# A layer of causal attention and gated FFN on 8 cores: squares moved to GpSimd, dequant jobs moved and paced anew inside attention, three output tiles moved to VectorE

## The chip, the cores and the metric

The kernel runs on the 8 cores of one Trainium2 chip. Each core takes one of 8 batch entries and computes it alone; no core talks to another. The metric is the device time in microseconds (us) of the slowest core. The engines are called PE (TensorE), DVE or VectorE, ACT or ScalarE, POOL or GpSimd, and SP (SyncE), which only issues DMAs here.

## The reference

```python
# per batch entry: x is [2048, 1024]
xn = layernorm(x)
q, k, v = xn @ Wq, xn @ Wk, xn @ Wv        # 16 heads of 64; rope on q and k
attn = softmax(causal(q @ k.T / 8))
s = (attn @ v) @ Wo
h = layernorm(xn) * gamma + beta
w1 = (fc1_q - 128) * fc1_scales            # int32 [1024, 4096], a scale per 128 rows
w2 = (fc2_q - 128) * fc2_scales            # int32 [4096, 1024]
f = xn + 0.5 * (silu(h @ w1 + b1) @ w2 + b2)
out = x + s * silu(f)
```

## The kernel before

The program is written as five blocks, b0 to b4, one after the other. In each block a small scheduler (`Sched`) keeps a list of instructions for every engine; `sch.op` adds one, `sch.wait` adds a wait for a semaphore count. Every engine executes its list strictly in the order in which the Python code has added to it, so the place of a call in the code is the place in the queue of each engine that it touches.

**b0 and b1** load constants, build the rope tables, compute the statistics of the rows and write the transposed, normalized input `xn_fm` (bf16).

**b2** projects. First V, while GpSimd multiplies (`emit_h_mul`, L397) and VectorE scales (`emit_h_ts`, L405) the eight slices of h. Then Q and K in eight slabs `it` (four each). A slab has four quarters `tgq` of 512 positions. For a quarter PE runs 16 matmuls (L558, L563), ACT copies both results out of PSUM (L574, L576), and VectorE does six rope instructions of 128x512 bf16 (L582 to L597), the first behind a wait for the copies of the slab before. At the slab's end ACT issues eight DMAs that place the result in `q_att` or `k_att` (L609, L612). The softmax needs a bound on the scores, for which the squared norms of each slab are summed. `emit_norm_sq(it-1)` puts the square of the first half of the slab before on ACT (L499), waiting for its eight DMAs, ahead of everything that ACT does for slab `it`. After quarter 1 of slab `it`, `emit_norm_mm(it-1, 0)` and `(it-1, 1)` follow: four PE matmuls with a vector of ones (L519), a VectorE reduce and maximum (L525, L533), for the second half first another square (L512). There is one buffer `nsq_b` and one PSUM bank for it, so the second square waits for the first norm's matmuls, and the second norm's matmuls wait for VectorE's maximum of the first. Quarters 2 and 3 stand behind them in PE's queue. After slab 7 the same is done with nothing beside it.

**b3** is attention, then the output projection and half of the first FFN matmul. Attention runs 32 groups: `qg` 0 to 3 (512 queries each) times `m` 0 to 7 (two heads each), with K = 4 qg + 4 key tiles. For each key tile `kt`, `emit_scores_exp` adds two score matmuls (L759), one exp on ACT (L778), and for the last four key tiles GpSimd's masks (memsets L788, multiplies L790). `emit_av(kt-2)` adds the matmuls with V (L808) and those that sum the softmax's denominators (L816); they wait for the masks. A group's epilogue has two parts. `ep_a` is two reciprocals of 1x512 (L829) and two casts (L834) on VectorE; it is added at kt = 1 of the next group. `ep_b` is two PE matmuls (L841), a copy (L849) and a multiply (L853) on VectorE; it is added at the end of the next group.

Beside attention the FFN weights are dequantized, in 48 jobs: 16 for w1 (2048 columns) and 32 for w2 (1024 columns). `emit_dq_job` adds two loads on SP, one scalar_tensor_tensor on VectorE (STT, L714), which waits for the loads and for the store of the job before, and the store on GpSimd (L719), which waits for the STT. All jobs use one set of buffers. At the end of each group, behind the epilogue of the group before, jobs are added until `want` are done; `gidx` is the number of groups added so far:

```python
                        if gidx <= 12:
                            want = min(ndq, gidx // 3)
                        else:
                            want = min(ndq, 4 + (gidx - 12) * (ndq - 4) // 20)
                        while dq_next < want:
                            emit_dq_job(dq_next)
```

**b4** does the second FFN matmul in two passes of eight row tiles (tile tt = 0 to 7 and 8 to 15) and, ahead of the second pass, the other half of the first FFN matmul (L1070, with Silu on ACT, L1078). For each row tile: PE's 64 matmuls (L1100, L1104), loads of x and s by SP (L1116, L1118), which wait until the two tiles before are computed (`o_done`), four VectorE instructions (L1125 to L1136), Silu on ACT (L1143), a multiply and an add, and the store issued by ACT. The multiply and the add are on GpSimd for tt < 13 (L1151, L1154) and on VectorE for 13 to 15 (L1159, L1162). The x tile and the result have two buffers each; the s tile has one.

Of the kernel before, what the change touches and what calls it, by code (L numbers as in the profile page):

```python
# [7 lines left out]
F32 = mybir.dt.float32  # L8
BF16 = mybir.dt.bfloat16
I32 = mybir.dt.int32  # L10
AF = mybir.ActivationFunctionType
# [3 lines left out]
S = 2048  # L15
D = 1024
# [77 lines left out]
def build_nc(upto=9):  # L94
# [31 lines left out]
    with ExitStack() as es:  # L126
# [5 lines left out]
        def sb(stack, name, cols, dt):  # L132
            return stack.enter_context(nc.sbuf_tensor(name, [128, cols], dt))
# [36 lines left out]
        with ExitStack() as ps:  # L170
# [4 lines left out]
            sch = Sched(cts)  # L175
# [51 lines left out]
        with ExitStack() as ps:  # L227
# [7 lines left out]
            sch = Sched(cts)  # L235
# [130 lines left out]
        with ExitStack() as ps:  # L366
# [5 lines left out]
            sch = Sched(cts)  # L372
# [78 lines left out]
            nsq_b = sb(ps, "nsq_b", S, BF16)  # L451
# [7 lines left out]
            dr_rep = {}  # L459
# [26 lines left out]
            sc_nsq = {}  # L486
            pe_nmm = {}
            ve_nrm = {}

            def emit_norm_sq(itx):  # L490
                ti_x, cp_x = itx // 4, itx % 4
                att_x = q_att if ti_x == 0 else k_att
                for j2 in range(2):
                    im = 8 * ti_x + 2 * cp_x + j2
                    m = 2 * cp_x + j2
                    if im >= 1:
                        sch.wait("scalar", "cPE", pe_nmm[im - 1])
                    sch.wait("scalar", f"dR{itx % 2}", dr_rep[(itx, 3)])
                    sch.op("scalar", lambda e, att_x=att_x, m=m: e.activation(  # L499
                        nsq_b[:], att_x[:, S * m:S * (m + 1)], AF.Square), inc="cSC")  # L500
                    sc_nsq[im] = sch.snap("cSC")
                    break

            def emit_norm_mm(itx, j2):
                ti_x, cp_x = itx // 4, itx % 4
                att_x = q_att if ti_x == 0 else k_att
                im = 8 * ti_x + 2 * cp_x + j2
                m = 2 * cp_x + j2
                if j2 == 1:
                    if im >= 1:  # L510
                        sch.wait("scalar", "cPE", pe_nmm[im - 1])
                    sch.op("scalar", lambda e, att_x=att_x, m=m: e.activation(  # L512
                        nsq_b[:], att_x[:, S * m:S * (m + 1)], AF.Square), inc="cSC")
                    sc_nsq[im] = sch.snap("cSC")
                sch.wait("tensor", "cSC", sc_nsq[im])
                if im >= 1:
# [22 lines left out]
            for ti, (w_d_, att) in enumerate(((wq_d, q_att), (wk_d, k_att))):  # L539
                for cp in range(4):  # L540
# [65 lines left out]
                    for j in range(4):  # L606
                        h = 4 * cp + j
                        m, r = h // 2, 64 * (h % 2)
# [40 lines left out]
        with ExitStack() as ps:  # L649
# [25 lines left out]
            with ExitStack() as ds:  # L675
# [46 lines left out]

                dq_next = 0
                sc_exp = {}
                pe_avl = {}
# [8 lines left out]
                for qg in range(NQG):  # L734
                    for m in range(8):
# [123 lines left out]
                        for kt in range(K):  # L859
                            emit_scores_exp(kt)  # L860
                            if kt == 1 and pending_ep[0] is not None:
                                pending_ep[0][0]()
                            if kt >= 2:
                                emit_av(kt - 2)
# [8 lines left out]
                        if gidx <= 12:  # L873
                            want = min(ndq, gidx // 3)
                        else:
                            want = min(ndq, 4 + (gidx - 12) * (ndq - 4) // 20)
                        while dq_next < want:
                            emit_dq_job(dq_next)
                            dq_next += 1
                pending_ep[0][0]()  # L880
# [137 lines left out]
        with ExitStack() as ps:  # L1018
# [5 lines left out]
            xb2 = [sb(ps, f"xb2_{i}", D, F32) for i in range(2)]  # L1024
            sb2 = [sb(ps, "sb2_0", D, F32)] * 2
            t_f = [sb(ps, f"t_f{i}", D, F32) for i in range(2)]
# [22 lines left out]
            for p in range(NP):  # L1049
# [35 lines left out]
                for ttl in range(8):  # L1085
# [59 lines left out]
                    sc_g[tt] = sch.snap("cSC")  # L1145
                    if tt < 13:
                        sch.wait("gpsimd", "cSC", sc_g[tt])
# [87 lines left out]
```

How the kernel before makes its waits and increments, by code:

```python
            def g(e, fn=fn, h=c.h, k=k):  # L49
                fn(e).then_inc(h, k)
# [4 lines left out]
    def wait(self, eng, name, val=None):  # L55
        c = self.ct[name]
        v = c.n if val is None else val
        self.streams[eng].append(lambda e, h=c.h, v=v: e.wait_ge(h, v))
```

## Time and profile before

| | us |
|---|---|
| median of 2 runs (1736.01 to 1739.34) | 1737.68 |
| profiled execution | 1737.32 |
| its span, core 3, the slowest | 1735.8 |
| spans of the eight cores | 1715.0 to 1735.8 |
| PE busy | 1170.3 |
| VectorE busy | 630.4 |
| ACT busy | 553.1 |
| GpSimd busy | 304.6 |

The granted TensorE clock has a mean of 0.829 to 0.835 on all cores. On the profile's page the busy shares are means over blocks with different limits. In the rows below the first number is the start in us from the span's beginning and the second the busy time; "x2" is a merged pair; in square brackets is how long the engine had been idle and what released it. Rows of a single line of code give the least, the middle and the greatest duration in ns.

### The profile page before, as it was taken

What the parts mean: (1) busy time and instruction counts of PE and PEld (TensorE: products, weight loads), DVE (VectorE), ACT (ScalarE), POOL (GpSimd) and SP (SyncE); (2) the same over time, 40 slices, a digit from 0 to 9 for tenths busy, and PEclk for the clock granted to TensorE, in tenths of its full rate; (3) what the DMA queues carried; (4) which work ended last, traced back from release to release, by engine and by line L of the source; (5) the groups of instructions that cost most, each with busy time, mean ns of one, the idle gap of its engine ahead of it and who ended that gap; (6) DMA issues with size and microseconds to landing.
All of it is one profiled execution on the core that took longest, in us unless ns stands there. A gap on an engine that the chain in (4) does not pass through costs nothing. (4 is left out here: it accounts for less than half of the span.)

```text
span 1735.8 us, 16309 instructions; the slowest of 8 cores (1715.0 to 1735.8 us)
## 1 busy us (share of the span) xinstructions
PE 1170.3 (67%) x5250; PEld 425.5 (25%) x5250; DVE 630.4 (36%) x674; ACT 553.1 (32%) x609; POOL 304.6 (18%) x574
## 2 busy tenths in 40 slices
PE   0004786456446675554777878838999997699994
PEld 0002332122111111111111212213444443244442
DVE  2132644334327875463556445531110112000123
ACT  1133002222324364333665767602222100243000
POOL 0100700000014333232222222220000123100230
PEclk9999898778765577666787877869999999799998
DMA  4645212322224114656444343356545322222213
GB/s 151 131 166 165 93 49 65 82 49 70 52 81 101 61 61 140 219 187 202 137 151 138 109 137 108 117 190 222 194 146 153 115 110 82 88 73 80 73 73 121
DMA packets 83923, 205.73 MB, mean 119 GB/s; under 512 B 16496, under 2 KB 33152, under 8 KB 78464
## 3 DMA queue, kind: packets, MB, share of 16 engines
q1 hardware_dynamic: 66096, 147.51, 26.9%
q10 hardware_dynamic: 8864, 29.38, 5.7%
q0 software_dynamic: 8880, 27.79, 5.1%
q8 instruction: 45, 0.74, 0.2%
q14 instruction: 38, 0.31, 0.1%
HBM read 163.21 MB, written 37.76 MB: 116 GB/s over the span
## 5 line engine op out<-in xcount | busy, mean ns | idle before, releaser
L778 ACT ACTIVATE ptb<-pbig,negub 128x1024 bf16<-128x1024 f32 x320 | 336.5, 1121 | 270.7 <-PE pbig L759 270.0
L808 PE MATMUL p<-ptb,v_tm 128*64 128x512 bf16 x640 | 162.8, 501 | 147.1 <-POOL ptb L788 92.2
L829 DVE RECIPROCAL lrec<-p 1x512 f32<-1x512 f32 x64 | 214.0, 3344 | 13.7 <-PE p L816 12.7
L759 PE MATMUL pbig<-q_att,k_att 64*128 64x512 bf16 x640 | 151.6, 488 | 35.3 <-ACT ptb L778 34.4
L816 PE MATMUL p<-ptb,ones_bf 128*1 128x512 bf16 x640 | 150.3, 466 | 0.0
L714 DVE SCALAR_TENSOR_TENSOR dq_o<-dq_i,dq_s 128x1024 bf16<-128x1024 int32 (+1 forms) x48 | 75.7, 1577 | 185.9 <-DMA w2deq<-dq_o 98.1
L1125 DVE TENSOR_SCALAR t_f<-xb,negmu_a,r_a 128x1024 f32<-128x1024 f32 x16 | 13.0, 813 | 337.0 <-PE p L1104 195.3
L946 PE MATMUL p<-h_fm,w1t 128*128 128x512 bf16 x512 | 118.6, 386 | 17.5 <-DMA w1t<-w1deq 11.4
L1070 PE MATMUL p<-h_fm,w1t 128*128 128x512 bf16 x512 | 112.6, 383 | 22.3 <-ACT y_sl L1078 22.3
L790 POOL TENSOR_TENSOR ptb<-ptb,msk_bf 128x128 bf16<-128x128 bf16 x256 | 112.1, 444 | 76.6 <-ACT ptb L778 76.4
L332 PE MATMUL pT<-idn_bf,xnb 128*128 128x128 bf16 x128 | 16.2, 306 | 150.6 <-DVE xnb L324 144.4
L1151 POOL TENSOR_TENSOR f_sb<-f_sb,sb 128x1024 f32<-128x1024 f32 x13 | 30.5, 2345 | 464.5 <-ACT f_sb L1143 464.5
L808 PEld LDWEIGHTS p<-ptb,v_tm 128*64 128x64 bf16 x640 | 40.8, 115 | 250.4 <-issue 250.4
L519 PE MATMUL p<-nsq_b,ones_bf 128*1 128x512 bf16 x64 | 29.8, 620 | 107.3 <-ACT nsq_b L499 68.0
L1143 ACT ACTIVATE f_sb<-f_sb 128x1024 f32<-128x1024 f32 x16 | 16.9, 1057 | 229.1 <-DVE f_sb L1136 229.1
L955 ACT ACTIVATE y_sl<-p,b_cm 128x512 bf16<-128x512 f32 x64 | 43.9, 687 | 125.5 <-PE p L946 125.5
L558 PE MATMUL pbig<-xn_fm,wE 128*128 128x512 bf16 x256 | 70.7, 426 | 2.9 <-DVE wO L481 2.9
L1070 PEld LDWEIGHTS p<-h_fm,w1t 128*128 128x128 bf16 x512 | 50.5, 99 | 84.3 <-issue 25.2
L946 PEld LDWEIGHTS p<-h_fm,w1t 128*128 128x128 bf16 x512 | 49.4, 99 | 84.6 <-issue 30.5
L1078 ACT ACTIVATE y_sl<-p,b_cm 128x512 bf16<-128x512 f32 x64 | 43.9, 687 | 72.4 <-PE p L1070 66.7
L759 PEld LDWEIGHTS pbig<-q_att,k_att 64*128 64x128 bf16 x640 | 31.7, 97 | 141.3 <-issue 141.3
L788 POOL MEMSET ptb<- 128x128 bf16 (+2 forms) x192 | 59.9, 312 | 20.7 <-ACT ptb L778 20.6
(138 smaller groups left out, 1511.8 us busy)
## 6 DMA issues: line engine op xcount, KB each, us to landing
xb<-x SPq DMA_DIRECT2D x48, 512.0 KB, 4.3
w1t<-w1deq SPq DMA_DIRECT2D x96, 256.0 KB, 2.7
dq_i<-fc_q SPq DMA_DIRECT2D x16, 1024.0 KB, 6.0
dq_s<-fc_scales SPq DMA_DIRECT2D x16, 1024.0 KB, 9.4
dq_i<-fc_q SPq DMA_DIRECT2D x32, 512.0 KB, 4.1
dq_s<-fc_scales SPq DMA_DIRECT2D x32, 512.0 KB, 5.1
w1deq<-dq_o POOLq DMA_DIRECT2D x16, 512.0 KB, 9.9
w2deq<-dq_o POOLq DMA_DIRECT2D x32, 256.0 KB, 5.6
```

The costliest lines, as they stand in the source:

```text
L558: sch.op("tensor", lambda e, fc=fc, tgq=tgq, pe_=pe_, wp=wp: e.matmul(pe_, wE[wp][:, 128 * fc:128 * (fc + 1)], xn_fm[:, S * fc + 512 * tgq ...
L714: sch.op("vector", lambda e, cols=cols, bi=bi: e.scalar_tensor_tensor(dq_o[bi][:, 0:cols], dq_i[bi][:, 0:cols], -128.0, dq_s[bi][:, 0:cols ...
L759: dst=(sc0 if jj == 0 else sc1): e.matmul(dst, k_att[r:r + 64, S * m + 128 * kt:S * m + 128 * (kt + 1)], q_att[r:r + 64, S * m + 512 * qg: ...
L778: sch.op("scalar", lambda e, pt=pt, half=half: e.activation(pt[:, 0:1024], pbig[:, 1024 * half:1024 * half + 1024], AF.Exp, bias=negub[:, ...
L788: sch.op("gpsimd", lambda e, pt=pt, base=base, off=off: e.memset(pt[:, base:base + off], 0.0), inc="cGP")
L790: sch.op("gpsimd", lambda e, pt=pt, base=base, off=off: e.tensor_mul(pt[:, base + off:base + off + 128], pt[:, base + off:base + off + 128 ...
L808: K=K, gp=gp: e.matmul(obank[gp][cpos:cpos + 64, :], v_tm[:, 1024 * kt + 64 * h:1024 * kt + 64 * (h + 1)], pt[:, 512 * (cpos // 64):512 * ...
L816: sch.op("tensor", lambda e, pt=pt, jj=jj, kt=kt, K=K, gp=gp: e.matmul(bass.AP(lbank[gp], 32 * jj * 512, [[512, 1], [1, 512]]), ones_bf[:] ...
L829: sch.op("vector", lambda e, jj=jj, gp=gp: e.reciprocal(lrec[32 * jj:32 * jj + 1, :], bass.AP(lbank[gp], 32 * jj * 512, [[512, 1], [1, 512 ...
L946: sch.op("tensor", lambda e, fc=fc, ph=ph, wb=wb, yp=yp: e.matmul(yp[:], wb[:, 128 * fc:128 * (fc + 1)], h_fm[:, S * fc + 512 * ph:S * fc ...
L955: sch.op("scalar", lambda e, oc=oc, ph=ph, yp=yp: e.activation(y_sl[:, 1024 * oc + 512 * ph:1024 * oc + 512 * (ph + 1)], yp[:], AF.Silu, b ...
L1070: sch.op("tensor", lambda e, fc=fc, ph=ph, wb=wb, yp=yp: e.matmul(yp[:], wb[:, 128 * fc:128 * (fc + 1)], h_fm[:, S * fc + 1024 + 512 * ph: ...
```

## The change

Three things are edited. In b2, all 16 squares become GpSimd multiplies. In b3, the dequant jobs that fall due at the end of a group are added in the next group at kt = 1, behind `ep_a` and ahead of the masks of kt = 2 and up, and from the 13th group on they are paced by 18 in place of 20. In b4, s gets a second buffer, and the multiply and add go to GpSimd for the first five tiles of each pass, which moves tiles 5, 6 and 7 to VectorE.

```diff
--- before.py
+++ after.py
@@ -490,16 +490,15 @@
             def emit_norm_sq(itx):
                 ti_x, cp_x = itx // 4, itx % 4
                 att_x = q_att if ti_x == 0 else k_att
-                for j2 in range(2):
-                    im = 8 * ti_x + 2 * cp_x + j2
-                    m = 2 * cp_x + j2
-                    if im >= 1:
-                        sch.wait("scalar", "cPE", pe_nmm[im - 1])
-                    sch.wait("scalar", f"dR{itx % 2}", dr_rep[(itx, 3)])
-                    sch.op("scalar", lambda e, att_x=att_x, m=m: e.activation(
-                        nsq_b[:], att_x[:, S * m:S * (m + 1)], AF.Square), inc="cSC")
-                    sc_nsq[im] = sch.snap("cSC")
-                    break
+                im = 8 * ti_x + 2 * cp_x
+                m = 2 * cp_x
+                if im >= 1:
+                    sch.wait("gpsimd", "cPE", pe_nmm[im - 1])
+                sch.wait("gpsimd", f"dR{itx % 2}", dr_rep[(itx, 3)])
+                sch.op("gpsimd", lambda e, att_x=att_x, m=m: e.tensor_mul(
+                    nsq_b[:], att_x[:, S * m:S * (m + 1)],
+                    att_x[:, S * m:S * (m + 1)]), inc="cGP")
+                sc_nsq[im] = sch.snap("cGP")
 
             def emit_norm_mm(itx, j2):
                 ti_x, cp_x = itx // 4, itx % 4
@@ -508,11 +507,12 @@
                 m = 2 * cp_x + j2
                 if j2 == 1:
                     if im >= 1:
-                        sch.wait("scalar", "cPE", pe_nmm[im - 1])
-                    sch.op("scalar", lambda e, att_x=att_x, m=m: e.activation(
-                        nsq_b[:], att_x[:, S * m:S * (m + 1)], AF.Square), inc="cSC")
-                    sc_nsq[im] = sch.snap("cSC")
-                sch.wait("tensor", "cSC", sc_nsq[im])
+                        sch.wait("gpsimd", "cPE", pe_nmm[im - 1])
+                    sch.op("gpsimd", lambda e, att_x=att_x, m=m: e.tensor_mul(
+                        nsq_b[:], att_x[:, S * m:S * (m + 1)],
+                        att_x[:, S * m:S * (m + 1)]), inc="cGP")
+                    sc_nsq[im] = sch.snap("cGP")
+                sch.wait("tensor", "cGP", sc_nsq[im])
                 if im >= 1:
                     sch.wait("tensor", "cVE", ve_nrm[im - 1])
                 for tgq in range(4):
@@ -721,6 +721,7 @@
                     dq_dg[ji] = sch.snap(f"dG{ji % 2}")
 
                 dq_next = 0
+                dq_quota = [0]
                 sc_exp = {}
                 pe_avl = {}
                 gp_msk = {}
@@ -860,6 +861,10 @@
                             emit_scores_exp(kt)
                             if kt == 1 and pending_ep[0] is not None:
                                 pending_ep[0][0]()
+                            if kt == 1:
+                                while dq_next < dq_quota[0]:
+                                    emit_dq_job(dq_next)
+                                    dq_next += 1
                             if kt >= 2:
                                 emit_av(kt - 2)
                         emit_av(K - 2)
@@ -871,12 +876,9 @@
                         gidx_c[0] += 1
                         gidx = gidx_c[0]
                         if gidx <= 12:
-                            want = min(ndq, gidx // 3)
+                            dq_quota[0] = min(ndq, gidx // 3)
                         else:
-                            want = min(ndq, 4 + (gidx - 12) * (ndq - 4) // 20)
-                        while dq_next < want:
-                            emit_dq_job(dq_next)
-                            dq_next += 1
+                            dq_quota[0] = min(ndq, 4 + (gidx - 12) * (ndq - 4) // 18)
                 pending_ep[0][0]()
                 pending_ep[0][1]()
                 pending_ep[0] = None
@@ -1022,7 +1024,7 @@
             p6 = ps.enter_context(nc.psum_tensor("p6_4", [128, 512], F32))
             p7 = ps.enter_context(nc.psum_tensor("p7_4", [128, 512], F32))
             xb2 = [sb(ps, f"xb2_{i}", D, F32) for i in range(2)]
-            sb2 = [sb(ps, "sb2_0", D, F32)] * 2
+            sb2 = [sb(ps, f"sb2_{i}", D, F32) for i in range(2)]
             t_f = [sb(ps, f"t_f{i}", D, F32) for i in range(2)]
             f_sb = [sb(ps, f"f_sb{i}", D, F32) for i in range(2)]
             w1t = [sb(ps, f"w1t{i}", NCH * 128, BF16) for i in range(3)]
@@ -1143,7 +1145,7 @@
                     sch.op("scalar", lambda e, fs=fs: e.activation(
                         fs[:], fs[:], AF.Silu), inc="cSC")
                     sc_g[tt] = sch.snap("cSC")
-                    if tt < 13:
+                    if ttl < 5:
                         sch.wait("gpsimd", "cSC", sc_g[tt])
                         sch.wait("gpsimd", f"dX{tt % 2}", dl_e)
                         if tt >= 2:
```

## Rows read from the trace of the kernel before

**Rows 1.** What PE's V matmuls (L808) waited for: releaser, total us, times

```profile
  POOL ptb L788: 92.2, 12
```

**Rows 2.** Timeline of VectorE, end of g14 to end of g15

```profile
725.15 0.69 DVE L849 COPY rep_sb<-p 128x512 f32<-128x512 f32 x1 [1.05 <-PE p L841]
...
726.78 2.29 DVE L714 SCALAR_TENSOR_TENSOR dq_o<-dq_i,dq_s 128x2048 bf16<-128x2048 int32 x1
739.97 2.29 DVE L714 SCALAR_TENSOR_TENSOR dq_o<-dq_i,dq_s 128x2048 bf16<-128x2048 int32 x1 [10.89 <-DMA w1deq<-dq_o]
742.17 6.72 DVE L829 RECIPROCAL lrec<-p 1x512 f32<-1x512 f32 x2
...
751.76 0.69 DVE L849 COPY rep_sb<-p 128x512 f32<-128x512 f32 x1 [1.73 <-PE p L841]
```

**Rows 3.** Timeline of GpSimd in g15, the first mask

```profile
743.97 0.81 POOL L790 TENSOR_TENSOR ptb<-ptb,msk_bf 128x128 bf16<-128x128 bf16 x2
```

**Rows 4.** Timeline of VectorE, ends of g28 and g29 (K=16)

```profile
1057.15 0.69 DVE L849 COPY rep_sb<-p 128x512 f32<-128x512 f32 x1 [3.76 <-PE p L841]
...
1080.02 0.69 DVE L849 COPY rep_sb<-p 128x512 f32<-128x512 f32 x1 [3.76 <-PE p L841]
```

**Rows 5.** Timeline of GpSimd in g29: a store's issue, the first mask

```profile
1068.55 0.54 POOL L719 DMA_DIRECT2D w2deq<-dq_o  x1 [7.66 <-DVE dq_o L714]
1072.83 0.80 POOL L790 TENSOR_TENSOR ptb<-ptb,msk_bf 128x128 bf16<-128x128 bf16 x2 [3.75 <-ACT ptb L778]
```

**Rows 6.** Timeline of VectorE: ends of g2, g3, g12, g17 and g30

```profile
544.28 0.69 DVE L849 COPY rep_sb<-p 128x512 f32<-128x512 f32 x1 [0.89 <-PE p L841]
...
557.82 0.69 DVE L849 COPY rep_sb<-p 128x512 f32<-128x512 f32 x1 [1.73 <-PE p L841]
...
670.00 0.69 DVE L849 COPY rep_sb<-p 128x512 f32<-128x512 f32 x1 [1.28 <-PE p L841]
...
816.67 0.69 DVE L849 COPY rep_sb<-p 128x512 f32<-128x512 f32 x1 [1.73 <-PE p L841]
...
1103.15 0.69 DVE L849 COPY rep_sb<-p 128x512 f32<-128x512 f32 x1 [4.89 <-PE p L841]
```

**Rows 7.** Timeline of VectorE behind g31, the last group

```profile
1126.80 1.22 DVE L714 SCALAR_TENSOR_TENSOR dq_o<-dq_i,dq_s 128x1024 bf16<-128x1024 int32 x1
1134.28 1.23 DVE L714 SCALAR_TENSOR_TENSOR dq_o<-dq_i,dq_s 128x1024 bf16<-128x1024 int32 x1 [6.26 <-DMA w2deq<-dq_o]
...
1144.13 6.72 DVE L829 RECIPROCAL lrec<-p 1x512 f32<-1x512 f32 x2
1150.95 0.86 DVE L834 CAST lrecb<-lrec 1x512 bf16<-1x512 f32 x2
```

**Rows 8.** Timeline of ACT: the first square of slab 3

```profile
375.32 1.91 ACT L499 ACTIVATE nsq_b<-q_att 128x2048 bf16<-128x2048 bf16 x1 [11.58 <-DMA q_att<-qo_s]
```

**Rows 9.** GpSimd's multiplies of h: durations in ns, minimum, median, maximum

```profile
L397 POOL TENSOR_TENSOR h_scr<-xn_fm,g_rep x8: 4043/4055/4063, 175.8 to 214.2; 128x2048 bf16<-128x2048 bf16 x8
```

**Rows 10.** Timeline of PE: both norms of slab 3

```profile
377.49 1.87 PE L519 MATMUL p<-nsq_b,ones_bf 128*1 128x512 bf16 x4 [8.07 <-ACT nsq_b L499]
384.93 1.86 PE L519 MATMUL p<-nsq_b,ones_bf 128*1 128x512 bf16 x4 [5.58 <-DVE stat L533]
```

**Rows 11.** Timeline of VectorE: the reduce between these norms

```profile
383.86 0.67 DVE L525 TENSOR_REDUCE stat<-p 1x1 f32<-1x512 f32 x1
```

**Rows 12.** The first rope multiply: durations in ns

```profile
L582 DVE TENSOR_TENSOR rp_t<-qeo,cos_sb x32: 417/425/427, 258.1 to 490.8; 128x512 bf16<-128x512 bf16 x32
```

**Rows 13.** VectorE's passes over h: durations in ns

```profile
L405 DVE TENSOR_SCALAR h_scr<-h_scr,gam_cm,bet_cm x8: 798/2594/4455, 179.9 to 220.0; 128x2048 bf16<-128x2048 bf16 x8
```

**Rows 14.** Groups of instructions: the multiply of b4 on GpSimd, on VectorE

```profile
L1151 POOL TENSOR_TENSOR f_sb<-f_sb,sb 128x1024 f32<-128x1024 f32 x13 | 30.5, 2345 | 464.5 <-ACT f_sb L1143 464.5
...
L1159 DVE TENSOR_TENSOR f_sb<-f_sb,sb 128x1024 f32<-128x1024 f32 x3 | 3.7, 1225 | 3.9 <-ACT f_sb L1143 3.9
```

**Rows 15.** Timeline of PE: restart behind the first pass of b4

```profile
1490.55 1.87 PE L1070 MATMUL p<-h_fm,w1t 128*128 128x512 bf16 x4 [22.32 <-ACT y_sl L1078]
```

## The prediction

> **What bounds the kernel now.** I read the table of cores first (all eight are alike, so one is enough), then the page's forty slices: PE's busy share is lowest from the second to the seventh tenth of the span, that is in the projections and in attention. So I opened these two stages.
>
> Attention (block b3) runs 32 groups, numbered 0 to 31 here; K, the number of key tiles in a group, is 4, 8, 12, 16 for eight groups each. The list of what PE waited for at L808 says that its largest idle time there was released by GpSimd's masks [rows 1]. To see why the masks are late, take one group, g15, in VectorE's timeline [rows 2]. I mark the end of a group by the COPY at L849, since it follows the group's last matmuls at once; e(g) is its start. e(14) is 725.15. 1.6 us later comes the first dequant job of the group (one STT at L714), the second follows 13.2 us after it, and says that it waited for the store of the first: there is one buffer. Only then come the two reciprocals, and e(15) is 751.76. GpSimd [rows 3] has to issue the second job's store, in order, ahead of g15's masks; the first mask starts at 743.97, 4.0 us after the second STT began, and e(15) follows 7.8 us behind. So the group's length is a sum:
>
> T = A + (n-1) s + c + t, where A is the time from e to the first STT (1.4 to 1.6), n the number of jobs, s their spacing (13.2 for a w1 job), c from the last STT to the first mask (4.0), t from the first mask to the end (7.8). 1.6+13.2+4.0+7.8 = 26.6, and 751.76 - 725.15 = 26.6.
>
> A w2 job is half as large: s is 7.5 (1126.80 to 1134.28 in [rows 7]); its STT is 1.2, its issue 0.5 [rows 5], with the wake-ups c = 2.4. Then T for n=2 is 1.4+7.5+2.4+7.4 = 18.7. In a K=16 group (g29, [rows 4, 5]) GpSimd had issued the store by 1069.1 and the first mask started only at 1072.83, released by ACT: 15.7 us after e(28) = 1057.15. There the masks aren't late, and the group's natural 22.9 us rules. At K=12 the two just meet, an estimate from the sum's own 18.7.
>
> **The change part by part.**
>
> *Dequant jobs go behind the reciprocals.* On VectorE the order was: jobs, reciprocals and casts, end of group. It becomes: reciprocals and casts, jobs, end of group. On GpSimd, for K above 4, nothing moves: the stores stay ahead of the group's masks. But each store waits for its STT, and the STT now has the reciprocals ahead of it: from the start of the first to the end of the casts 1144.13 to 1151.81 [rows 7], 7.7 us. Before, these 7.7 us ran beside the masks and the last matmuls (t is 7.8): hidden. Now they are in A, which is 1.4+7.7 = 9.1. What is queued behind the waiting stores are the masks; who waits for those is PE. SP's loads keep their place: a load is issued as soon as the STT before it is done.
>
> Early jobs, one each, at g3, g6, g9, g12, as before. K=8: 9.1+4.0+7.8 = 20.9, against 13.2 by the same sum with A=1.4, of which the natural length may cover a little: I take +7 each, 14 for the two. K=4: half the masks are ahead of the store, so t is shorter, an estimate of 4.9: 18.0, against 557.82-544.28 = 13.5 [rows 6]: +9 for two.
>
> *The pace.* want becomes 4 + (gidx-12)*44//18, run in group gidx. That gives n = 2,2,3,2,3 in g13 to g17 (12 w1 jobs), then 2,3,2,3,2,2,3,2,3,2,3,2,3 w2 jobs in g18 to g30, none in g31.
>
> g13 to g17: three at 9.1+13.2+4.0+7.8 = 34.1 and two at 47.3, together 196.9. Before: 816.67-670.00 = 146.7 [rows 6]. +50.2.
>
> g18 to g30: seven with n=2 at 9.1+7.5+2.4+7.4 = 26.4, six with n=3 at 33.9: 388.2. Release of the masks is now e+19.0 for n=2, so even K=16 (15.7) waits. Before: 1103.15-816.67 = 286.5. +101.7.
>
> *The tail.* Three jobs stood between the end of g31 and the last reciprocals: STTs from 1126.80, reciprocals from 1144.13 [rows 7]. With all jobs done by g30 the reciprocals start where the first STT did: -17.3. g31 itself is natural either way.
>
> Attention: 9+14+50.2+101.7-17.3 = **+158 us**.
>
> *Squares go from ACT to GpSimd* (16, two per slab; seven slabs are followed by another). An ACT square takes 1.91 [rows 8]; GpSimd's multiply of the same shape, L397, takes 4.06 [rows 9]. Let D be the landing of the slab's copies (375.32, when the square of [rows 8] starts). PE's first norm matmuls start at D+2.2 and last 1.87; the second ones start at D+9.6 [rows 10], and release came from VectorE: its reduce started at 383.86, 1.07 us ahead [rows 11]. So ACT's second square had slack. By GpSimd alone: 4.06, 0.3, 2.0 for the first norm, 4.06, 0.3 = D+10.7: +1.1 per slab, 8 for seven, and 2 x 2.15 = 4.3 behind the last slab, where nothing covers: **12**. The ACT queue becomes free sooner, and its evacuations run sooner, but PE stands behind the norm matmuls, so I cost that gain at nothing.
>
> The other end: VectorE's 12 rope multiplies of two quarters also wait for D (425 ns each, 5.3 us with overlap and gaps [rows 12]) and would run beside GpSimd's square. No row of before shows such a pair. The nearest is L405, a VectorE pass over the same tile: 0.80 alone and 4.46 when a GpSimd multiply of 4.06 ran beside it [rows 13]: it stood still for the whole of that instruction. If the rope does so too: square 0 to 4.1; rope 4.1 to 6.3; second square 6.3 to 10.4; the 3.1 of rope that is left to 13.5; 1.1 for reduce, maximum and wake-up: D+14.6, or 14.9 if the first rope instruction gets in ahead of the square. I take D+14.8, +5.2 per slab: 36, and 4.3: **40**. The unlucky order (rope wholly ahead of the first square) would give D+16, 49 in all. I take 40, as the only row of the kind shows a full stop, and keep 12 and 49 as bounds.
>
> The Trainium skill ("SBUF — State Buffer", section "Who interferes with whom") says that a VectorE instruction with two SBUF inputs and a GpSimd instruction that reads SBUF exclude each other for a whole instruction, and that whichever starts first goes on. The row of L405 shows the exclusion only for a one-input pass; by the rule the sum is the 40, without it the 12.
>
> *Second sb2 buffer.* SP's loads of a tile still wait for o_done of both tiles before, so nothing starts sooner: 0. It isn't hidden by anything; the wait is simply left in.
>
> *Tiles 5 to 7 of b4 on VectorE.* The multiply takes 2.35 on GpSimd and 1.23 on VectorE [rows 14], and I take the add to be as long: 2.4 per tile with hand-overs, between 2.2 and 2.6. VectorE is idle then. These tiles form a chain: output done, load of the next tile, t_f, Silu, output; PE is ahead of it and stood 22.3 us for ACT's first y_sl, which is queued behind tile 7's output [rows 15]. So three tiles give 3 x 2.4 = **-7**, all of it on the path.
>
> **Sum.** 158+40-7 = +191, on the profiled execution's 1737.3 (its span 1735.8): 1928. The median shown is 1737.7, the same within 0.4. Forecast: 1928.
>
> **The rivals.**
> - *No exclusion in b2.* Everything else as above: 1900. For: no row of two-input VectorE work beside GpSimd. Against: L405.
> - *Two-job groups stay hidden.* If at K=12 and 16 the masks with n=2 came in time after all, four groups lose 7.7 less and three 3.5 less: -41, 1887. Against: T = 18.7 meets the K=12 lengths of before closely, so there is no slack to use.
> - *Not slower (other side).* One mechanism: job spacing shrinks. Stores may land sooner when PE and DMA are less loaded. The new order has 7 w1 and 19 w2 spacings, 7x13.2+19x7.5 = 235 us; to give back 191 they would have to fall by 80%, to under 3 us. Then 1737. Against: the wait is for a store and a load each, both much longer than that.
> - *Colder PE.* Every stall is followed by matmuls at the lower clock level, as in t of [rows 3] (7.8) against 7.2 in [rows 4, 5]. If all 13 late groups take 7.8 and the b2 order is the unlucky one: +5 and +9, 1942; contention of denser jobs might bring 1955.
>
> **How the numbers follow.** Likeliest (1928, own range 1905 to 1945) 0.70; no exclusion 0.14; hidden two-job groups 0.06; colder or more contended 0.08; not slower 0.02. The range 1890 to 1955 leaves out part of the hidden case and the last. A measurement of this kernel tells 2% (35 us) from no change; every case but one is over 1772. Faster 0.01, same 0.02, slower 0.97.
>
> **What would show it.** In the changed profile: reciprocals at e+1.4 in every group and the first STT at e+9.1; masks late by 7.7 at K=8 and 12; groups of 34 and 47, then 26 and 34 us; PE's wait for masks at L808 about doubled or more; no STT after the last group; 4.06 us squares with rope instructions stretched to 4 us beside them; PE's wait at L1070 down from 22 to 15. I am wrong if the masks start as early as before, or if job spacing changes.

## Result, and the profile after

The changed kernel takes 1928.0 us (median; 1916.8 to 1954.7), against 1733.4 for the kernel before on the same chip. The ratio is 1.112, with a 95% interval of 1.109 to 1.114. The 1954.7 is an execution in which some cores were granted a lower clock (0.76 and 0.77 on its two slowest), and the ratios leave such executions out. The profiled execution of after has a span of 1924.3 us on core 5, and all eight cores lie between 1895.1 and 1924.3.

The page of after shows first where the time is. Busy time by engine (share of the span, instructions), PE's busy tenths and its granted clock in forty slices:

```profile
PE 1188.5 (62%) x5250; PEld 426.3 (22%) x5250; DVE 680.3 (35%) x680; ACT 524.4 (27%) x593; POOL 345.6 (18%) x584
...
PE   0016856445454674233645566685799999699995
...
PEclk9999977767755665566666676776899999899998
```

PE does the same 5250 matmuls, and the end of the kernel (the nines) looks as before; what is thin is the stretch of slices 7 to 26. The groups of instructions on the page, and what PE waited for at the V matmuls (the line is L809 now, it was L808):

```profile
L809 PE MATMUL p<-ptb,v_tm 128*64 128x512 bf16 x640 | 171.5, 530 | 313.2 <-POOL ptb L789 255.4
...
L719 POOL DMA_DIRECT2D w2deq<-dq_o x32 | 17.9, 558 | 300.1 <-DVE dq_o L714 300.1
```

The wait for GpSimd's first masks rose from 92.2 us in 12 waits [rows 1] to 255.4, in 21. The second row names the cause one step further back: GpSimd itself stood 300.1 us ahead of the 32 w2 stores, waiting for VectorE's dequant instruction, and the masks are in its queue behind the stores. Ahead of all 48 stores it was 499.7 us, where before it was 302.6.

One group, g14 (K=8, two jobs), in VectorE's timeline, from one end mark to the next:

```profile
760.13 0.69 DVE L850 COPY rep_sb<-p 128x512 f32<-128x512 f32 x1 [8.95 <-PE p L842]
...
761.54 6.71 DVE L830 RECIPROCAL lrec<-p 1x512 f32<-1x512 f32 x2
...
769.25 2.29 DVE L714 SCALAR_TENSOR_TENSOR dq_o<-dq_i,dq_s 128x2048 bf16<-128x2048 int32 x1
783.90 2.29 DVE L714 SCALAR_TENSOR_TENSOR dq_o<-dq_i,dq_s 128x2048 bf16<-128x2048 int32 x1 [12.36 <-DMA w1deq<-dq_o]
795.99 0.69 DVE L850 COPY rep_sb<-p 128x512 f32<-128x512 f32 x1 [9.79 <-PE p L842]
```

and GpSimd and PE in the same group:

```profile
787.20 1.15 POOL L719 DMA_DIRECT2D w1deq<-dq_o  x1 [13.92 <-DVE dq_o L714]
788.37 0.81 POOL L791 TENSOR_TENSOR ptb<-ptb,msk_bf 128x128 bf16<-128x128 bf16 x2
789.33 0.64 PE L809 MATMUL p<-ptb,v_tm 128*64 128x512 bf16 x2 [21.07 <-POOL ptb L789]
```

The terms can be read off: A = 769.25 - 760.13 = 9.1, spacing 14.65, the second STT 783.90, PE's V matmuls go on at 789.33, the end at 795.99: 35.9 us. In the group of [rows 2, 3], g15 with two jobs as well, the STTs came ahead of the reciprocals, and it took 26.6.

The end marks at the borders of the parts, to be laid beside [rows 6, 7]:

```profile
575.09 0.69 DVE L850 COPY rep_sb<-p 128x512 f32<-128x512 f32 x1 [0.89 <-PE p L842]
593.13 0.69 DVE L850 COPY rep_sb<-p 128x512 f32<-128x512 f32 x1 [6.63 <-PE p L842]
...
725.27 0.69 DVE L850 COPY rep_sb<-p 128x512 f32<-128x512 f32 x1 [9.37 <-PE p L842]
...
923.42 0.69 DVE L850 COPY rep_sb<-p 128x512 f32<-128x512 f32 x1 [8.65 <-PE p L842]
...
1315.57 0.69 DVE L850 COPY rep_sb<-p 128x512 f32<-128x512 f32 x1 [8.71 <-PE p L842]
1337.96 0.69 DVE L850 COPY rep_sb<-p 128x512 f32<-128x512 f32 x1 [13.31 <-PE p L842]
...
1347.94 0.69 DVE L850 COPY rep_sb<-p 128x512 f32<-128x512 f32 x1 [0.89 <-PE p L842]
```

These are e(2), e(3), e(12), e(17), e(30), e(31) and the last end. Part by part, in us (core 5 of after, core 3 of before):

| part of attention | before | after | difference | forecast |
|---|---|---|---|---|
| g3 to g12, e(2) to e(12) | 125.7 | 150.2 | +24.5 | +23 |
| g13 to g17 | 146.7 | 198.2 | +51.5 | +50.2 |
| g18 to g30 | 286.5 | 392.2 | +105.7 | +101.7 |
| g31 and the last epilogue | 49.6 | 32.4 | -17.2 | -17.3 |
| all, e(2) to the last end | 608.4 | 772.9 | +164.4 | +158 |

The cores differ among themselves: each compared with itself, the last row is between +152 and +170 on the eight cores.

The rest of the kernel, on core 5 of both: the norm matmuls of b2 lie between 274.3 and 503.2 before, and between 274.3 and 538.9 after, so +35.7 us. From the first matmul of the output projection to the end it is 580.2 before and 574.7 after, so -5.5. The whole span of core 5 is 1729.0 before and 1924.3 after: +195.3, of which the stretch from the first Exp to the output projection holds 165.2, b2 35.7, and the rest -5.5.

b2, slab 3 of after. GpSimd's two squares, and what VectorE does beside them:

```profile
382.52 3.60 POOL L498 TENSOR_TENSOR nsq_b<-q_att 128x2048 bf16<-128x2048 bf16 x1 [27.02 <-DMA q_att<-qo_s]
382.55 4.11 DVE L481 CAST wO<-wstg 128x1024 bf16<-128x1024 f32 x1 [6.60 <-DMA wstg<-wk]
...
386.37 1.86 PE L519 MATMUL p<-nsq_b,ones_bf 128*1 128x512 bf16 x4 [9.76 <-POOL nsq_b L498]
...
388.38 3.81 POOL L511 TENSOR_TENSOR nsq_b<-q_att 128x2048 bf16<-128x2048 bf16 x1 [2.27 <-PE p L519]
388.83 3.63 DVE L597 TENSOR_TENSOR qo_s<-rp_t 128x512 bf16<-128x512 bf16 x1
...
396.40 1.87 PE L519 MATMUL p<-nsq_b,ones_bf 128*1 128x512 bf16 x4 [8.17 <-DVE stat L533]
```

A rope instruction of 0.42 us takes 3.63 beside the second square, and the cast of a weight, 0.69 us elsewhere, takes 4.11 beside the first. The rope instruction ends 0.3 us behind its square and the cast 0.5 behind its own: each got on only when the square was done. PE's second norm starts 13.9 us after the slab's copies, where before it was 9.6 [rows 10], and it is released by VectorE. What PE waited for at L519, in all (us, times, by releaser):

```profile
  POOL nsq_b L498: 85.7, 8
  DVE stat L533: 41.4, 6
```

Both waits grew: before they were 68.0 (on ACT's square) and 26.5.

### The profile page after: what moved, and what is told of

Its sections match the earlier page's. It is cut to its first block and busy times, and to the rows that moved or that the text cites. A ratio compares the mean times of both kernels' runs of the same rounds, so it can differ in the third digit from the quotient of the medians.

```text
span 1924.3 us, 16303 instructions; the slowest of 8 cores (1895.1 to 1924.3 us)
## 1 busy us (share of the span) xinstructions
PE 1188.5 (62%) x5250; PEld 426.3 (22%) x5250; DVE 680.3 (35%) x680; ACT 524.4 (27%) x593; POOL 345.6 (18%) x584
## 5 line engine op out<-in xcount | busy, mean ns | idle before, releaser
L809 PE MATMUL p<-ptb,v_tm 128*64 128x512 bf16 x640 | 171.5, 530 | 313.2 <-POOL ptb L789 255.4
L830 DVE RECIPROCAL lrec<-p 1x512 f32<-1x512 f32 x64 | 213.9, 3342 | 13.5 <-PE p L817 12.5
L760 PE MATMUL pbig<-q_att,k_att 64*128 64x512 bf16 x640 | 155.8, 501 | 35.8 <-ACT ptb L779 34.9
L817 PE MATMUL p<-ptb,ones_bf 128*1 128x512 bf16 x640 | 156.6, 485 | 0.0
L809 PEld LDWEIGHTS p<-ptb,v_tm 128*64 128x64 bf16 x640 | 40.9, 118 | 424.0 <-issue 424.0
L791 POOL TENSOR_TENSOR ptb<-ptb,msk_bf 128x128 bf16<-128x128 bf16 x256 | 108.2, 429 | 73.0 <-ACT ptb L779 72.7
L519 PE MATMUL p<-nsq_b,ones_bf 128*1 128x512 bf16 x64 | 29.8, 620 | 142.7 <-POOL nsq_b L498 85.7
L1153 POOL TENSOR_TENSOR f_sb<-f_sb,sb 128x1024 f32<-128x1024 f32 x10 | 23.5, 2346 | 471.9 <-ACT f_sb L1145 471.9
L850 DVE COPY rep_sb<-p 128x512 f32<-128x512 f32 x32 | 22.1, 692 | 224.2 <-PE p L842 223.2
L574 ACT ACTIVATE qeo<-pbig 128x512 bf16<-128x512 f32 x32 | 19.2, 598 | 235.6 <-PE pbig L563 158.1
L957 ACT ACTIVATE y_sl<-p,b_cm 128x512 bf16<-128x512 f32 x64 | 44.0, 687 | 128.4 <-PE p L948 126.5
L719 POOL DMA_DIRECT2D w2deq<-dq_o x32 | 17.9, 558 | 300.1 <-DVE dq_o L714 300.1
```

What stands on the lines that cost most here:

```text
L760: dst=(sc0 if jj == 0 else sc1): e.matmul(dst, k_att[r:r + 64, S * m + 128 * kt:S * m + 128 * (kt + 1)], q_att[r:r + 64, S * m + 512 * qg: ...
L791: sch.op("gpsimd", lambda e, pt=pt, base=base, off=off: e.tensor_mul(pt[:, base + off:base + off + 128], pt[:, base + off:base + off + 128 ...
L809: K=K, gp=gp: e.matmul(obank[gp][cpos:cpos + 64, :], v_tm[:, 1024 * kt + 64 * h:1024 * kt + 64 * (h + 1)], pt[:, 512 * (cpos // 64):512 * ...
L817: sch.op("tensor", lambda e, pt=pt, jj=jj, kt=kt, K=K, gp=gp: e.matmul(bass.AP(lbank[gp], 32 * jj * 512, [[512, 1], [1, 512]]), ones_bf[:] ...
L830: sch.op("vector", lambda e, jj=jj, gp=gp: e.reciprocal(lrec[32 * jj:32 * jj + 1, :], bass.AP(lbank[gp], 32 * jj * 512, [[512, 1], [1, 512 ...
```

## The experiments

Each kernel is the kernel before with only the edit shown, unless it says otherwise. Ratios are against the kernel before on the same chip, whose medians were 1739 to 1745 us, so 0.01 of a ratio is 17.4 us.

### One part at a time

**The squares alone.** Both squares of a slab are multiplies on GpSimd, as in the change:

```
-  sch.op("scalar", ... e.activation(nsq_b[:], att_x[...], AF.Square), inc="cSC")
+  sch.op("gpsimd", ... e.tensor_mul(nsq_b[:], att_x[...], att_x[...]), inc="cGP")
```

> The kernel before with only the 16 squares moved to GpSimd. Theory (GpSimd's square and VectorE's two-input rope instructions exclude each other): about +36 us, some 1769, and in the trace one or two rope instructions per slab stretched to 3.6 us or more. Rival (no exclusion, only the slower square counts): +12 us, 1745, all rope instructions near 425 ns.

Measured: 1.0164 (1.0113 to 1.0216), that is +29 us (20 to 38). The norms take 263.6 us from the first matmul to the last, against 227.9 before on the core shown there, and PE waited at L519 for 86.4 us (squares) and 41.4 us (VectorE), as in after. This kernel's slab 3 shows the rope multiply itself stopped, where in after the cast happened to be there:

```profile
383.06 3.71 POOL L498 TENSOR_TENSOR nsq_b<-q_att 128x2048 bf16<-128x2048 bf16 x1 [27.86 <-DMA q_att<-qo_s]
383.23 3.82 DVE L582 TENSOR_TENSOR rp_t<-qeo,cos_sb 128x512 bf16<-128x512 bf16 x1
...
389.03 3.73 POOL L511 TENSOR_TENSOR nsq_b<-q_att 128x2048 bf16<-128x2048 bf16 x1 [2.27 <-PE p L519]
389.22 3.82 DVE L582 TENSOR_TENSOR rp_t<-qeo,cos_sb 128x512 bf16<-128x512 bf16 x1
```

The multiply of 0.43 us starts 0.2 us behind the square and ends 0.3 us behind it. So it is in each of the 14 squares that run beside a following slab: one rope instruction is stopped by each, and all that VectorE has queued waits behind it. It works the other way too. A square that started first took 3.60 us; where a VectorE cast or rope instruction was already running when the square was released, the square took up to 4.12 us and ended 3.5 us behind the end of that instruction. The 12 us that GpSimd's own slowness would give lie outside the interval.

**The same waits, but GpSimd reads nothing.** The squares are left out, so the norms of this kernel are not the real ones; in the place of each, two memsets write 128x2048 elements each, behind the same waits:

```
+  sch.op("gpsimd", lambda e: e.memset(ms_b[:], 1.0), inc="cGP")
+  sch.op("gpsimd", lambda e: e.memset(nsq_b[:], 1.0), inc="cGP")
```

> The squares on GpSimd are left out: in their place GpSimd writes a constant with two memsets of 128x2048 (some 3.5 us together), which read nothing; the norms are then a constant, and the bound of the softmax with them. All waits are those of the kernel with the squares moved. Theory (the exclusion needs a GpSimd instruction that reads SBUF): rope instructions stay near 425 ns, and block b2 is at most 8 us longer than before. Rival (any long GpSimd instruction stops VectorE): rope instructions stretched to the memset's length, b2 longer by some 30 us.

Measured: 1.0064 (1.0042 to 1.0086), +11 us, a little above what was expected. Slab 3:

```profile
376.41 2.31 POOL L500 MEMSET ms_b<- 128x2048 bf16 x1 [22.50 <-DMA q_att<-qo_s]
376.89 0.42 DVE L583 TENSOR_TENSOR rp_t<-qeo,cos_sb 128x512 bf16<-128x512 bf16 x1
```

and the rope multiplies and the weight casts over the whole stage (minimum/median/maximum in ns):

```profile
L583 DVE TENSOR_TENSOR rp_t<-qeo,cos_sb x32: 406/422/426, 257.8 to 494.5; 128x512 bf16<-128x512 bf16 x32
...
L482 DVE CAST wO<-wstg x8: 683/694/2176, 247.8 to 442.7; 128x1024 bf16<-128x1024 f32 x8
```

No rope multiply is stopped (maximum 426, with the squares 3852), though GpSimd is busy for as long. One cast is: 2176 ns against 694. Where a cast was running first, the memset waited: that is why the one above took 2.31 us, while one that met no cast took 1.80. The rule of the Trainium skill ("SBUF — State Buffer", section "Who interferes with whom") is that a VectorE instruction with two SBUF inputs contends only with a GpSimd instruction that reads SBUF, and that copies and casts in a two-port mode contend with any. These two runs and their numbers agree with both halves. So of the +29, about 11 come from GpSimd's length, and the rest from the exclusion of VectorE. This split is an estimate, since two memsets (3.6 us together, up to 4.2 where one of them had to wait) and a square (3.7) are not quite the same length.

**The order alone.** The jobs go behind the reciprocals, and the pace stays:

```
+  if kt == 1:
+      while dq_next < dq_quota[0]:
+          emit_dq_job(dq_next); dq_next += 1
...
-  while dq_next < want: ...
+  dq_quota[0] = min(ndq, 4 + (gidx - 12) * (ndq - 4) // 20)
```

> The kernel before with only the place of the dequant jobs changed (behind the reciprocals), pace still 20. Theory: every group with n jobs lasts 9.1+(n-1)s+c+t; g13 to g17 34 us each and 47 for the last, K=12 and 16 groups 26.4 with two jobs; sum about +138 us, 1871. Rival (the reciprocals' place is neutral and the pace does the harm): within 10 us of before.

Measured: 1.0832 (1.0784 to 1.0881), +145 us. A is 9.1 in every group with a job but g15, where it is 9.5. A K=16 group with two w2 jobs in VectorE's timeline:

```profile
1105.03 0.69 DVE L850 COPY rep_sb<-p 128x512 f32<-128x512 f32 x1 [7.86 <-PE p L842]
...
1114.15 1.23 DVE L714 SCALAR_TENSOR_TENSOR dq_o<-dq_i,dq_s 128x1024 bf16<-128x1024 int32 x1
1121.58 1.23 DVE L714 SCALAR_TENSOR_TENSOR dq_o<-dq_i,dq_s 128x1024 bf16<-128x1024 int32 x1 [6.21 <-DMA w2deq<-dq_o]
1131.53 0.69 DVE L850 COPY rep_sb<-p 128x512 f32<-128x512 f32 x1 [8.73 <-PE p L842]
```

It takes 26.5, as the sum for n=2 says (26.4), where such a group took 22.9 before [rows 4]. The moving of the jobs is most of the change's cost, and the rival that two-job groups stay hidden has fallen. One thing was not foreseen. In this kernel the last three jobs run behind the last epilogue, which is therefore short (9.97 us). The gain is not kept: all engines but PE wait for the last job's store before they go on, so that PE stands in the output projection for VectorE's copies:

```profile
1302.28 1.23 DVE L714 SCALAR_TENSOR_TENSOR dq_o<-dq_i,dq_s 128x1024 bf16<-128x1024 int32 x1 [7.72 <-DMA w2deq<-dq_o]
1307.92 0.58 PE L968 MATMUL p<-wo_bf,o_sb 128*128 128x512 bf16 x1 [12.54 <-DVE s_st L983]
```

From the last end to the first FFN matmul it is 42.6 us here, where before it was 20.4. So the stretch up to the last end is 130.8 us longer than before, and these 22 us come on top.

**The pace alone.** `// 18` in the place of `// 20`, with the jobs at their old place:

> The kernel before with only the pace changed from 20 to 18, jobs still ahead of the reciprocals. Theory: g13 to g17 +13, g18 to g30 +14, tail -17, so about +9 us, 1742. Rival (the pace is what makes the change slow): +50 us or more.

Measured: 1.0079 (1.0049 to 1.0108), +14 us. Attention, e(2) to the last end, is 11.5 us longer than before on the cores shown (6, and 3 before).

**Order and pace together.** The two single effects add to 1.0911. They need not add: the faster pace spares the new order the three jobs behind the last epilogue, and makes more groups with three jobs, each longer in the new order. So the pair was run by itself:

> Order of the jobs and pace together, squares and tiles as before. If the masks behind the late stores make the attention stage and the parts simply coexist, attention is the +164 us that the changed kernel's trace shows, so this is the kernel before + 164, a ratio of 1.095 (1.090 to 1.099); with the squares alone (1.0164) and the tiles alone (0.9937) the sum is then 1.105 to 1.11, the changed kernel. If order and pace do not interact, their single effects add: 1.0832 + 0.0079 = 1.091, and some 10 us of the changed kernel would stay unexplained. The trace decides where 4 us of time can't: every extra w2 job should cost 7.5 us in the new order also at K = 16, where in the old order it was partly hidden.

Measured: 1.094 (1.0887 to 1.0993), +164 us (155 to 173), and by its trace +162.9 from e(2) to the last end. The attention part of the changed kernel was +164.4 by its trace. The interval doesn't exclude 1.091. The trace does show what the pace costs in the new order: in K=16 groups g27 takes 26.4 with two jobs and g28 34.1 with three, 7.7 more, where with the pace alone the K=16 groups with three jobs take 26.1 to 27.4 against the natural 22.9, 3.2 to 4.5 more.

**The b4 edits alone.** Tiles 5 to 7 on VectorE, and the second `sb2` buffer:

```
-  if tt < 13:
+  if ttl < 5:
```

> The kernel before with only the changes of the last block: the second sb2 buffer, and tiles 5 to 7 on VectorE. Theory: -7 to -9 us, about 1725, all of it from PE's wait ahead of its restart at the second pass (22 us to 14). Rival (the chain of tiles is not what PE waits for): no change.

Measured: 0.9937 (0.9906 to 0.9968), -11 us. The first matmul of the second pass, with its wait:

```profile
1482.34 7.98 PE L1070 MATMUL p<-h_fm,w1t 128*128 128x512 bf16 x29 [14.56 <-ACT y_sl L1078]
```

22.3 [rows 15] became 14.6. This run doesn't tell the second buffer from the tiles; that the buffer gives nothing here is read from the code, where the loads still wait for both tiles before.

The parts add up within their noise: 0.0164 + 0.0940 - 0.0063 = 0.104, and the three intervals together leave some 0.008, against 0.112 (0.109 to 0.114) for the whole. The 13 us between them are not placed.

### What stands in the way: stores, or reciprocals

**Stores off GpSimd, in the new order.** The kernel has the changed order and pace. The job stores are issued by SP, so nothing stands ahead of the masks on GpSimd:

```
-  sch.op("gpsimd", ... e.dma_start(out=dsth, in_=dq_o[bi][:, 0:cols]), ...)
+  sch.op("sync",   ... e.dma_start(out=dsth, in_=dq_o[bi][:, 0:cols]), ...)
```

> The kernel before with order and pace of the dequant jobs as changed, but the stores of the jobs issued by SP, so that the masks on GpSimd have nothing ahead of them. Theory (the change is slow only because masks queue behind stores that wait for VectorE): groups fall to VectorE's own length, 24.7 and 37.9 us for two and three w1 jobs, 18.5 or natural for two w2 jobs, 25.3 for three; attention about 10 us shorter than before, total near 1728. Rival (VectorE or the DMAs themselves make it slow): over 1850, as with the stores on GpSimd.

Measured: 1.0046 (1.002 to 1.0072), +8 us, where some 10 us less than before were expected. Most of the +164 is gone, and with it the wait for masks; what PE waited for at L809:

```profile
PE p L809 <- DVE o_sb L854: 108.2, 8, 32.8
...
PE p L809 <- POOL ptb L791: 74.2, 101, 2.8
```

The longest wait for a mask is 2.8 us (in the changed kernel they average 12). So the cost of the new order does come through GpSimd's queue. (The stores also land sooner when SP issues them; the next run speaks against this as the cause, since the spacing of the jobs stays there.) In its place PE waits for VectorE's epilogue, 108.2 us in eight waits, 94.7 of it in the five behind g13 to g17. There the COPY of the group's end stands behind the group's last w1 job on VectorE, as in g13:

```profile
699.51 2.29 DVE L714 SCALAR_TENSOR_TENSOR dq_o<-dq_i,dq_s 128x2048 bf16<-128x2048 int32 x1 [13.72 <-DMA dq_s<-fc_scales]
701.84 0.69 DVE L850 COPY rep_sb<-p 128x512 f32<-128x512 f32 x1
```

On the core shown (7, the slowest), the spacing was 15.8 to 16.3 us in g13, g14 and at the start of g15, and 13.8 at its end. On cores 3 and 5 it was 12.2 to 13.2, and their spans are 1711.9 and 1723.5 against 1755.0; the time of a run is that of the slowest core. Why core 7's loads landed later stays open.

**Stores off GpSimd, in the old order.** To see whether SP's queue lengthens the spacing, the same edit on the kernel before:

> The kernel before with the stores of the dequant jobs issued by SP instead of GpSimd, nothing else. With order and pace changed as well (the earlier run) the spacing of w1 jobs was 15.8 to 16.3 us instead of 13.2. If the SP queue causes that (the next job's loads are behind a store in its order), the spacing here is again about 16 us, w1 jobs still end up off the masks' path, and the time falls because GpSimd's masks no longer stand behind stores: attention 40 to 90 us shorter, total 1650 to 1700 us. If the spacing came from the new order, it is 13 here.

Measured: 0.9963 (0.9937 to 0.999), -6.5 us, where 40 to 90 were expected. The spacing is 12.5 to 13.1, so SP's queue isn't what lengthened it. But g15 is still 26.4 us long, in VectorE's timeline:

```profile
716.83 0.69 DVE L849 COPY rep_sb<-p 128x512 f32<-128x512 f32 x1 [0.89 <-PE p L841]
...
719.30 2.29 DVE L714 SCALAR_TENSOR_TENSOR dq_o<-dq_i,dq_s 128x2048 bf16<-128x2048 int32 x1 [0.99 <-DMA dq_s<-fc_scales]
732.42 2.29 DVE L714 SCALAR_TENSOR_TENSOR dq_o<-dq_i,dq_s 128x2048 bf16<-128x2048 int32 x1 [10.83 <-DMA dq_s<-fc_scales]
734.63 6.72 DVE L829 RECIPROCAL lrec<-p 1x512 f32<-1x512 f32 x2
...
743.21 0.69 DVE L849 COPY rep_sb<-p 128x512 f32<-128x512 f32 x1 [0.89 <-PE p L841]
```

and what PE waited for in attention:

```profile
PE p L841 <- DVE lrecb L834: 108.0, 19, 25.1
PE p L808 <- POOL ptb L790: 66.2, 99, 2.7
```

The masks are in time, but PE now waits at L841 for the reciprocals, which stand behind the second job on VectorE. In the kernel before, two queues end their work at about the same time: the store ahead of the masks on GpSimd, and the job ahead of the reciprocals on VectorE. To free one of them is worth 6.5 us. The change freed VectorE's and thereby made GpSimd's 7.7 us later.

**Both freed at once.** If that is right, the jobs have to go where neither the masks nor the reciprocals stand behind a wait. Here they are 64 jobs of 1024 columns, and the same space holds two sets of buffers. None run in the K=4 groups, then 2, 3 and 3 per group; the first at the old place, the others behind the reciprocals and behind the group's last masks:

```
+  if kt == K - 1:
+      while dq_next < dq_late[0]:
+          emit_dq_job(dq_next); dq_next += 1
...
+  njobs = (0, 2, 3, 3)[gidx // 8] if gidx < 32 else 0
```

> The kernel before with the dequant jobs cut to 1024 columns each (64 jobs), two sets of buffers in the same space, none in the groups with K=4, then 2, 3 and 3 per group: one at the old place, the others behind the reciprocals and, on GpSimd, behind the group's last masks. Theory (the 80 us of stall in g13 to g27 and the 17 us of tail are all waits for a buffer): groups at their natural lengths of 10, 14, 18.5 and 22.5 us, attention 70 us shorter, total near 1665. Rival (DMA bandwidth is the limit): groups of K=8 stay over 20 us and the gain is under 30 us.

Measured: 0.9504 (0.9471 to 0.9536), -86 us. The K=16 groups take 20.0 to 22.8 us with three jobs in each; this is g30:

```profile
1013.70 0.69 DVE L847 COPY rep_sb<-p 128x512 f32<-128x512 f32 x1 [9.90 <-PE p L839]
...
1015.10 1.22 DVE L711 SCALAR_TENSOR_TENSOR dq_o<-dq_i,dq_s 128x1024 bf16<-128x1024 int32 x1
1016.24 6.72 DVE L827 RECIPROCAL lrec<-p 1x512 f32<-1x512 f32 x2
...
1023.95 2.36 DVE L711 SCALAR_TENSOR_TENSOR dq_o<-dq_i,dq_s 128x1024 bf16<-128x1024 int32 x2
1033.68 0.69 DVE L847 COPY rep_sb<-p 128x512 f32<-128x512 f32 x1 [7.36 <-PE p L839]
```

The two late jobs run back to back (x2, 2.36 us) without waiting for a store. The stores are still on GpSimd, and attention from e(2) to the last end is 522.6 us, against 608.4. This kernel changes size, buffering and place together, so it doesn't tell what each is worth; it shows that the waits, and not the work, set attention's length.

**The second `sb2` buffer really used.** The b4 edits, and the loads of a tile wait only for the output of the tile before last:

```
-  for k in (tt - 1, tt - 2):
+  for k in (tt - 2,):
```

> The kernel before with tiles 5 to 7 of b4 on VectorE, two sb2 buffers, and the loads of a tile waiting only for the output of the tile before last. If the loads were on the chain, the wait of PE before the second pass falls from 14 us (tiles alone) to about 6, and the waits inside the chain shrink: 20 to 25 us less than tiles alone, 1700 to 1710 us. If the second buffer is worth nothing even with the wait lifted, this equals tiles alone: a ratio of 0.994.

Measured: 0.9799 (0.9766 to 0.9832), -35 us, 24 more than the b4 edits alone; PE's wait ahead of the second pass is 5.6 us. So the wait that was left in was worth 24 us, and lifting it needs the second buffer. How much of it came from the loads of x, which had two buffers already, and how much from those of s, no run separates.

**All that helped, together.** The spread jobs and this:

> The spread jobs, tiles 5 to 7 on VectorE, and the second sb2 buffer put to use: the loads of a tile wait only for the tile two before. Theory: the chain of the last block breaks, PE's wait ahead of the second pass falls from 22 us to under 5 and the end moves up by 10 us; about 34 us less than the spread jobs alone, total near 1630. Rival (PE is the limit of that block anyway): 8 us less, as with the tiles alone.

Measured: 0.9303 (0.9264 to 0.9341), 1619.0 us. It is faster than both kernels: some 120 us less than before on the same chip, and 309 less than the changed kernel, measured on another. The two gains, 86 and 35, add.

## Why the prediction was right

*The sum.* It said 1928 and the median is 1928.0. That the two meet to the microsecond is luck. The forecast of the change was +191 on 1737, and measured were +194.6 on 1733.4; the parts are off by more than that, and their errors cancel.

*Attention, +158; shown +164.4 (152 to 170 by core).* The formula held term by term: A is 9.1 in all groups with jobs but two (9.5 in g15 and g30), the masks were late in all of them, and groups of 18.0 and 20.8 us (forecast 18.0 and 20.9) appear in K=4 and K=8. The order alone gave 26.5 for a two-job K=16 group, with 26.4 forecast. The missing 6 us are nearly all in the spacings, which had been taken from one row each: the seven w1 spacings were 12.9 to 14.6 us, 94.7 in all (13.2 each gives 92.4), and the nineteen w2 spacings 7.3 to 8.6, 145.7 in all (7.5 each gives 142.5). That the cost runs through the stores on GpSimd is shown by moving the stores to SP, which took nearly all of it back.

*Squares, +40; shown +29 by time (20 to 38) and +36 by the stage's length.* The right bound was chosen: VectorE's two-input instructions stand still while GpSimd's multiply reads, and do not beside a memset. The size was a little high. A square took 3.6 to 3.8 us and not 4.06; the row it was priced by multiplies two tensors and the square one with itself, which may be why, but no run shows it. The second norm started 13.9 us behind the slab's copies in slab 3 and 12.9 to 13.9 in the seven slabs, with 14.8 forecast; before it was 9.2 to 9.6. That the cast of a weight is stopped too wasn't in the working.

*Second buffer, 0.* No run has the buffer alone. With the wait lifted, it and the tiles are worth 35 us together, against 11 with the wait left in, which fits.

*Tiles, -7; shown -11 (-6 to -16).* PE's wait fell by 8.7 in after and by 7.8 in the run of this edit alone. That is 2.6 to 2.9 per tile, where 2.4 was taken.

*The rivals.* "No exclusion" fell with the memsets, "hidden two-job groups" with the order alone, "not slower" with the spacings, which rose and did not shrink. "Colder PE" is in part true: the granted clock fell from 0.83 to 0.80 as a mean over the core. But the tails t of the 13 groups g18 to g30 are 7.5 us in the mean, where the sum had 7.4 and this rival 7.8; in g14 t is 7.6 (788.37 to 795.99), where the sum had 7.8.

*What the working didn't see.* It had the two lengths side by side, 7.7 us of reciprocals and a tail of 7.8, but described the old order as held by GpSimd alone. The run with the stores on SP shows that the reciprocals on VectorE were only just behind: the same 26.4 us stand with the masks in time. For the forecast it made no difference, since the change made the GpSimd side later; for anyone who wants to mend the kernel it does.

## What to carry to other kernels

An in-order queue that issues a store after a wait delays all that stands behind it, so before moving a producer down its own engine's stream, look at which engine issues its store and what stands behind that. When a wait is removed and the time stays, look for a second queue that ends its work at the same moment, and free both. Before work goes to GpSimd, look for VectorE instructions with two SBUF inputs, and casts like the one here, that will run beside it, and price VectorE as stopped for the whole length of each GpSimd instruction that reads SBUF and meets one.

## What the runs showed of the hardware

- A VectorE instruction of 0.42 us with two SBUF inputs took 3.6 to 3.85 us beside a GpSimd multiply of 3.6 to 3.8, and 0.42 beside a memset.
- A VectorE cast from f32 to bf16 (0.69 us) took 4.11 beside the multiply, and 2.18 beside a memset in the one case in which the memset started first: it is stopped by a GpSimd instruction that only writes also. Where the cast ran first, the memset (1.80 us) took 2.0 to 2.3.
- GpSimd's multiply of a 128x2048 bf16 tile with itself took 3.60 us when it started first, up to 4.12 when it was released while a VectorE cast or rope instruction was running, and that of two tiles 4.06 [rows 9].
- The w1 stores (512 KB) landed 4.1 us (median) after they were issued when SP issued them and 9.9 when GpSimd did, both in the old order, and yet the spacing of the jobs stayed at 13: with SP the wait of the STT was for the load of the scales.
